# A one-layer language-model tower: two-pass attention scores on whole-number rows, and a new order of a turn

## The reference, cut to what matters

```python
def _L0_attn_ref(x, Wq, bq, Wk, bk, Wv, bv, Wo, bo, gamma, beta):
    q = jnp.einsum('bsd,dhk->bshk', x, Wq) + bq
    k = jnp.einsum('bsd,dhk->bshk', x, Wk) + bk
    v = jnp.einsum('bsd,dhk->bshk', x, Wv) + bv
    scores = jnp.einsum('bqhk,bshk->bhqs', q, k) * scale
    attn = jax.nn.softmax(scores, axis=-1)
    ctx = jnp.einsum('bhqs,bshk->bqhk', attn, v)
    attn_out = jnp.einsum('bqhk,hkd->bqd', ctx, Wo) + bo
    y = x + attn_out
    return (y - mu) * jax.lax.rsqrt(var + EPS) * gamma + beta      # mu, var of y

h = _L0_tok_ref(x, mask, ...)                 # embedding, window features, fusion, layer norm
h = h + _L0_attn_ref(_layernorm(h), ...)
h = h + _L0_ffn_ref(_layernorm(h), ...)       # top-2 gate, each expert takes 64 rows, GELU
return h
```

## Time and profile before

| what | value |
|---|---|
| median of 3 runs | 537.13 us |
| lowest and highest of the runs | 536.72 and 547.7 us |
| time of the profiled execution | 537.01 us |
| its span, from the first to the last instruction | 535.2 us |
| mean granted TensorE clock, as a share of full speed | 0.989 |
| TensorE matmul busy (share of the span) | 497.3 us (93%) |
| DVE busy | 447.9 us (84%) |
| GpSimd busy | 384.7 us (72%) |
| ScalarE busy | 379.2 us (71%) |

### The profile page before, as it was taken

How to read it: one execution, slowest core, us unless ns; L and a number is a source line. 1 busy time by engine, 2 the same in 40 slices (tenths; PEclk the granted TensorE clock), 3 DMA queues, 4 the chain that set the end, 5 groups by cost and what they waited for, 6 DMA issues and landing times. The chain is left out here.

```text
span 535.2 us, 15239 instructions
## 1 busy us (share of the span) xinstructions
PE 497.3 (93%) x5567; PEld 362.8 (68%) x5567; DVE 447.9 (84%) x1054; ACT 379.2 (71%) x768; POOL 384.7 (72%) x519
## 2 busy tenths in 40 slices
PE   5988799999999999999999998769999999999984
PEld 3876567777777777776777775534466767777664
DVE  4797669999999999998999999868778898878675
ACT  2868778888898888988898887336766555556530
POOL 1025669888788888888888888750468798789783
PEclk9998989999999999999999999999999999999998
DMA  6800000000000000000000000000734163351011
GB/s 233 333 6 2 2 2 4 2 3 3 3 2 3 3 3 3 4 2 4 3 4 2 3 3 2 2 1 4 168 80 100 23 150 76 77 138 38 31 40 60
DMA packets 11902, 21.68 MB, mean 41 GB/s; under 512 B 4668, under 2 KB 9780, under 8 KB 10164
## 3 DMA queue, kind: packets, MB, share of 16 engines
q1 hardware_dynamic: 11410, 20.15, 13.8%
q10 hardware_dynamic: 418, 0.55, 0.4%
HBM read 16.24 MB, written 4.33 MB: 38 GB/s over the span
## 5 line engine op out<-in xcount | busy, mean ns | idle before, releaser
L845 POOL TENSOR_TENSOR s_pl<-s_pf,s_ph 128x512 f16<-128x512 f32 x128 | 147.0, 1160 | 8.7 <-ACT s_ph L959 8.7
L1062 DVE TENSOR_REDUCE s_mx<-ps 128x4 f32<-128x512 f32 x128 | 83.8, 677 | 17.6 <-PE ps L1225 14.1
L953 ACT ACTIVATE s_pf<-ps,s_ln_r 128x512 f32<-128x512 f32 x128 | 87.1, 683 | 11.4 <-PE ps L1238 8.9
L823 PE MATMUL ps<-s_xt_all,s_w1s 128*128 128x512 f16 x384 | 87.9, 379 | 2.2 <-ACT s_ub L1543 1.6
L1698 PE MATMUL ps<-s_w2s,s_hid 128*128 128x256 f16 x768 | 88.9, 273 | 0.0
L1698 PEld LDWEIGHTS ps<-s_w2s,s_hid 128*128 128x128 f16 x768 | 75.1, 98 | 11.0
L959 ACT ACTIVATE s_ph<-s_pf 128x512 f16<-128x512 f32 x128 | 74.0, 637 | 0.0
L1273 PE MATMUL ps<-s_zh,s_cth 128*128 128x256 f16 x256 | 69.9, 273 | 1.0 <-DVE s_ctl L1096 1.0
L1273 PE MATMUL ps<-s_zl,s_cth 128*128 128x256 f16 x256 | 69.8, 273 | 0.0
L1273 PE MATMUL ps<-s_zh,s_ctl 128*128 128x256 f16 x256 | 69.8, 273 | 0.0
L823 PEld LDWEIGHTS ps<-s_xt_all,s_w1s 128*128 128x128 f16 x384 | 37.3, 98 | 41.4 <-ACT s_ub L1543 2.1
(11 more groups left out here) (246 smaller groups left out, 1149.0 us busy)
## 6 DMA issues: line engine op xcount, KB each, us to landing
s_rep<-picks SPq DMA_DIRECT2D x14, 512.0 KB, 6.7
s_stage<-in_w SPq DMA_DIRECT2D x2, 1024.0 KB, 14.3
out<-s_zh SPq DMA_DIRECT2D x16, 128.0 KB, 2.0
out<-s_lg SPq DMA_DIRECT2D x16, 128.0 KB, 1.7
s_stage<-in_wq SPq DMA_DIRECT2D x1, 1024.0 KB, 5.0
s_stage<-in_wk SPq DMA_DIRECT2D x1, 1024.0 KB, 6.7
s_stage<-in_wv SPq DMA_DIRECT2D x1, 1024.0 KB, 8.3
s_stage<-in_wo SPq DMA_DIRECT2D x1, 1024.0 KB, 10.8
```

What stands on the lines that cost most here:

```text
L823: mm = nc.tensor.matmul(hidden_bank(n)[:], w1s[:, wp, c, j * P:(j + 1) * P], xt_all[:, GB * g:GB * (g + 1), xp, c, :], start=(k == 0), sto ...
L845: nc.gpsimd.tensor_tensor(flat(pl[:, b % 2, 4 * j:4 * j + 4, :]), pf[:, j, :], flat(ph[:, b % 2, 4 * j:4 * j + 4, :]), ALU.subtract).then_ ...
L953: nc.scalar.activation(pf[:, j, :], ST[j % 2][:], ACT.Exp, bias=ln_r[:, b:b + 1]).then_inc(exp_done[j], 1)
L1062: nc.vector.tensor_reduce(mx[:, b % 2, c:c + 4], A[ab][:].rearrange("p (h k) -> p h k", h=4), AX.X, ALU.max).then_inc(max_done[hf][ab], 1)
```

## The change

The three passes of `score_cols` become two. The stationary operand is no longer the scaled `ub` in two parts but `nkT`, the transposed whole-number counts, which one float16 holds exactly. The key's scale moves into the exponential, as `scale=r12` of the activation. Three scale vectors are carried as pairs of rows (a float16 and its rest), so the row numbers `ONE` and `SHIFT` move, and `SHIFT` is now two rows. The transfers of `mrow` become four in a turn instead of two.

`nkT` is made in block one: eight `nkt_part` groups of eight matmuls, which take the place of both stretches of `keep_going`, four copies on ScalarE and four on DVE. The copy of `nb` to `nk` on ScalarE moves to behind the wo biases. The scale rows of `nkT` are filled at the start of block two: four small matmuls (`scale_rows`), one copy on DVE, and twelve transfers of 32 rows of 256 bytes each on SyncE's queue, ahead of the first `mrow` transfers.

The order of a turn changes on three engines. On TensorE `score_rows(i+3, 1)` now stands behind `residual(i)` where `score_rows(i+4, 1)` stood at the end of the turn, the second half of `q_rows` comes first, and `maxima_cols` stands between the two halves. On ScalarE `q_hi(1)` comes before `max_row`, and `probs_hi(1)` moves to the start of the next turn. On DVE both `q_lo` are at the start of the turn and `y_scaled` comes before the second half's `sum_root`.

```diff
-R2, ONE, SHIFT = 2 * V, 2 * V + 1, 2 * V + 2
-ONE_HI, UV = R2 + 2, R2 + 4
+R2, ONE, SHIFT = 2 * V, 2 * V + 2, 2 * V + 4
+UV = ONE + 2
...
+                def nkt_cols(n):
+                    dve.wait_ge(nt_ready, 8 + n + 1)
+                    nc.vector.tensor_copy(nkT[:, 16 + 4 * n:20 + 4 * n, :].rearrange("p b t -> p (b t)"), NKT_BANKS[4 + n][:])\
+                        .then_inc(nkt_ok, 1)
...
+                sp.wait_ge(srow_step, 2)
+                for ab in range(2):
+                    for r, j in ((R2, 0), (R2 + 1, 1), (ONE, 2), (ONE + 1, 3), (SHIFT, 2), (SHIFT + 1, 3)):
+                        r += ab * UD
+                        sp.dma_start(nkT[r:r + 1, :, :], srow[:, j, :]).then_inc(in_srow, 16)
                 for b in range(B):
                     sp.wait_ge(mrow_done, b + 1)
                     for ab in range(2):
-                        r = ab * UD + SHIFT
-                        sp.dma_start(qh[r:r + 1, b % 2].rearrange("o f t q -> o (f t) q"),
-                                     mrow[8 * ab:8 * ab + 8, b % 2, :]).then_inc(shift_in[b % 2], 16)
+                        for r in range(ab * UD + SHIFT, ab * UD + SHIFT + 2):
+                            sp.dma_start(qh[r:r + 1, b % 2].rearrange("o f t q -> o (f t) q"),
+                                         mrow[8 * ab:8 * ab + 8, b % 2, :]).then_inc(shift_in[b % 2], 16)
...
-                    nc.scalar.activation(pf[:, j, :], ST[j % 2][:], ACT.Exp, bias=ln_r[:, b:b + 1]).then_inc(exp_done[j], 1)
+                    nc.scalar.activation(pf[:, j, :], ST[j % 2][:], ACT.Exp, bias=ln_r[:, b:b + 1], scale=r12[:, b:b + 1]).then_inc(exp_done[j], 1)
...
 # ScalarE's order of a turn
+                    if has(i + 2) and i > -2:
+                        probs_hi(i + 2, 1)
                     if has(i + 1):
                         context_hi(i + 1, 0)
+                    if has(i + 2):
+                        exps(i + 2, 3)
...
                     if has(i + 4):
-                        q_hi(i + 4, 0)
+                        q_hi(i + 4, 1)
...
                     elif has(i + 3):
                         max_row(i + 3)
-                    if has(i + 2):
-                        exps(i + 2, 3)
                     if has(i + 4):
-                        q_hi(i + 4, 1)
+                        q_hi(i + 4, 0)
...
                 def score_cols(b, hf):
                     if hf == 0:
-                        pe.wait_ge(shift_in[b % 2], 32 * (b // 2) + 32)
+                        pe.wait_ge(shift_in[b % 2], 64 * (b // 2) + 64)
+                        if b == 0:
+                            pe.wait_ge(in_srow, 16 * 12)
...
-                    for n, (part, q) in enumerate(((0, qh), (0, ql), (1, qh))):
+                    for n, q in enumerate((qh, ql)):
                         for ab in range(2):
                             r = slice(ab * UD, ab * UD + UD)
-                            mm = nc.tensor.matmul(ST[ab][:], ub[r, b, part, :], flat(q[r, b % 2, hf]),
-                                                  start=(n == 0), stop=(n == 2))
+                            mm = nc.tensor.matmul(ST[ab][:], nkT[r, b, :], flat(q[r, b % 2, hf]),
+                                                  start=(n == 0), stop=(n == 1))
...
 # TensorE's order of a turn
+                scale_rows()
                 for i in STEPS:
                     if has(i):
                         residual(i)
+                    if has(i + 3):
+                        score_rows(i + 3, 1)
+                    tokens(i - 1, 2)
+                    if has(i - 1):
+                        logits(i - 1)
                     if has(i + 1):
+                        values(i + 1, 1)
                         turn(i + 1, 0)
-                        values(i + 1, 1)
                     if i == B:
                         first_hidden(4)
-                    if has(i - 1):
-                        logits(i - 1)
+                    if has(i + 2):
+                        score_cols(i + 2, 1)
                     if i == -3:
                         maxima_cols(0)
                     if has(i + 4):
-                        q_rows(i + 4, 0)
-                    if has(i + 2):
-                        score_cols(i + 2, 1)
+                        q_rows(i + 4, 1)
                     if has(i + 3) and i > -3:
                         maxima_cols(i + 3)
+                    if has(i + 4):
+                        q_rows(i + 4, 0)
                     if has(i + 1):
                         turn(i + 1, 1)
-                    if has(i + 4):
-                        q_rows(i + 4, 1)
...
-                    if has(i + 4):
-                        score_rows(i + 4, 1)
-                    tokens(i, 2)
```

More of the change, by code:

```diff
@@ L581, in _, with nkt_part @@
                         mm.then_inc(nt_ready, 1)
-                keep_going(15, psum[0][:, 0:FREE])
+                def nkt_part(n):
+                    if 1 <= n < 4:
+                        pe.wait_ge(nt_ok, (1, 2, 4)[n - 1])
+                    elif n >= 4:
+                        pe.wait_ge(nt_ok, 4 + (2, 3, 1, 4)[n - 4])
+                    for k in range(4):
+                        for ab in range(2):
+                            mm = nc.tensor.matmul(NKT_BANKS[n][ab * UD:(ab + 1) * UD, k * P:(k + 1) * P], nb[:, 4 * n + k, :], ident16[:],
+                                                  start=True, stop=True)
+                    mm.then_inc(nt_ready, 1)
+                for n in range(4):
+                    nkt_part(n)
                 pe.wait_ge(in_id, 16)
@@ L590, in _ @@
                 tp.then_inc(mt_ready, 1)
-                keep_going(6, psum[0][:, 0:FREE])
+                nkt_part(4)
+                nkt_part(5)
                 pe.wait_ge(mt_ok, 1)
@@ L1137, in _ @@
                         q_lo(i + 5, 1)
[L1138 to L1139 removed]
+                        q_lo(i + 5, 0)
+                    if i == -4:
+                        log_rho()
+                    elif i < -4:
+                        for n in DVE_TOKENS.get((i, 0), ()):
+                            token_rows(n)
                     if has(i + 2):
                         context_lo(i + 2, 1)
[L1142 to L1143 removed]
                     if has(i + 3):
@@ L1166, in _ @@
                         sums(i + 3, 1)
-                    if has(i + 1) and i % 4 == 2:
-                        logits_out((i + 1) // 4)
+                    if has(i + 2):
+                        y_scaled(i + 2)
                     if has(i + 3):
@@ L1171, in _ @@
                         context(i + 3, 1)
-                    if has(i + 2):
-                        y_scaled(i + 2)
-                    if has(i + 3):
                         context_lo(i + 3, 0)
-                    if has(i + 6):
-                        q_lo(i + 6, 0)
                     if has(i + 2):
@@ L1300, in logits, with scale_rows @@
                     mm.then_inc(lg_ready, 1)
+                def scale_rows():
+                    for j in range(4):
+                        mm = nc.tensor.matmul(MISC[0:B, j * P:(j + 1) * P], nk[:, :, R2 + j:R2 + j + 1].rearrange("p b o -> p (b o)"),
+                                              identh[:], start=True, stop=True)
+                    mm.then_inc(srow_step, 1)
                 def maxima_cols(b):
+                    if b == 0:
+                        pe.wait_ge(srow_step, 2)
                     for n in range(2):
```

80 lines of the change are left out of this document (49 added, 31 removed).

## The result

The changed kernel takes 589.16 us (median of 4 runs, 583.69 to 594.37) against 539.67 for the kernel before, a ratio of 1.090 (95% interval 1.077 to 1.104). Its profiled execution took 583.69 us, with a span of 581.9.

The account below looks back on a forecast made before the run. The prediction took SyncE's queue of four transfers to set a 9.63 us turn: 537.0 profiled + 33.0 for thirty turns + 1.1 block one + 0 start + 0.8 last sequence = 571.9, so 572 us; range 557 to 600.

Parts of the forecast that it names:

- the queue's loop: From `q_rows(1)` over SyncE's four `mrow` transfers and the scores to the next `q_rows(1)`: 9.63 us a turn; 74%.
- 30 ordinary turns against 8.53: Turns between second and last `mrow`: each 1.10 us longer, 33.0 us in all.
- up to the second `mrow`: Block one +1.1 us, for four DVE copies ahead of `quads`; start of block two counted 0.
- last `mrow` to the router's transposes: The last sequence: `max_row` to scores grows from 2.88 to 4.08 us; less two passes, +0.8.
- X: Landing time from the start of the last `mrow` issue to the scores: 1.75 us, possible from 1.30 to 2.10.
- both "hidden" rivals: The four transfers don't set the turn: DVE's loop does, 535 us (9%), or a shorter DVE loop, 525 us (5%).
- `q_rows(1)` to `q_hi(1)`: First step of the queue's loop, until ScalarE's input is ready: 0.65 us.
- the clock falls: TensorE's clock falls for good through its 1.5 us stall in every turn: over 750 us; 3%.
- the slow start: Twelve scale-row transfers in block two cost up to 2.7 us each and hold the first scores: 594 us; 9%.
- GpSimd's at 8.50: Old turn's loop from `residual` through GpSimd to `x_cols` and back: 8.50 us, falling to 8.08 with the change.
- DVE's at 8.40: Old turn's loop from `score_rows(1)` through DVE's maxima and `context_lo(0)` to `output(0)` and back: 8.40 us, unchanged.
- TensorE alone: TensorE's own loop of starts in a turn: 8.50 us before, 8.06 with one pass less in each half.

Follow-up runs that it names:

- before_four: The kernel before, with each `mrow` transfer issued twice, the extra one to a tile nobody reads: four transfers in a turn; ratio 1.072, turn 9.70 to 9.71 us.
- after_one_row: The changed kernel with two `mrow` transfers in a turn, leaving out the low part of the row maxima's scale: 538.4 us, ratio 0.9997, turn 8.44.
- after_two_queues: The changed kernel with two of the four `mrow` transfers issued by ScalarE right behind `max_row`: 582.8 us, ratio 1.083, turn 9.89.
- after_const_scale: The changed kernel with a constant instead of the column of key scales in the exponentials: 578.9 us, ratio 1.074, turn 9.68.
- after_one_row_best: `after_one_row` with `max_row` ahead of `q_hi(1)` and `first_hidden(4)` ahead of the last `logits`: 528.6 us, ratio 0.982, turn 8.22.
- before_residual_first: The kernel before with only `score_rows(1)` moved behind `residual`, three passes and two transfers: 540.5 us, ratio 1.004, turn 8.56.

## Why the prediction was right, and where its size was off

The forecast was 572 us, slower, by the queue's loop; it came out slower, inside the range, by that loop. The profiled execution took 583.7, so 11.8 more than the sum. The turn of 9.77 instead of 9.63 comes from one mis-sized term; most of the rest was not in the sum at all:

| part | forecast | measured | off by |
|---|---|---|---|
| 30 ordinary turns against 8.53 | 33.0 | 30 x 1.24 = 37.2 | +4.2 |
| irregular turns | 0 | 301.0 - 293.1 = 7.9 | +7.9 |
| up to the second `mrow` | +1.1 | 66.14 - 68.88 = -2.7 | -3.8 |
| last `mrow` to the router's transposes (at 411.0, before 364.7) | +0.8 | 43.9 - 40.0 = +3.9 | +3.1 |
| the rest | 0 | 170.9 - 170.5 = +0.4 | +0.4 |

- *The queue's terms held.* 128 transfers, 0.63 to issue the median one, four in 2.64; X was 1.76 where I took 1.75. `before_four` and `after_one_row` show that they are the cause, and both "hidden" rivals fall.
- *The rule of the Trainium skill.* "DMA: Bandwidth & Descriptors", section "Issuing engines are not separate DMA queues", calls the time to start a DMA usually small relative to the DMA. The measured turn doesn't agree for transfers this small: 0.66 against a landing of 1.76. The same section's other half, that a second engine saves just this time on the sequencer, agrees with `after_two_queues`, where two queues issued side by side (1.30 and 1.40 for two each).
- *Mis-sized: `q_rows(1)` to `q_hi(1)`.* I took 0.65; it was 0.79. The exponential that stands between them got the scale column and takes 778 ns instead of 689. I costed only the passes, transfers and orders of the diff, and not the operand it added to `exps`. `after_const_scale` gives back 0.09. The page "ScalarE: Activation LUTs", section "What ACT_TABLE_LOAD costs", states about 93 ns for each column operand; the trace agrees with 0.09.
- *Missed: irregular turns.* The forecast took an ordinary turn times 30. Before, most of a late transfer fell into slack, and 30 turns cost 0.85 more than 30 x 8.50 in all. Now nothing covers it: what lands late is added in full, and behind three of the pauses the clock was halved for some microseconds, 1.6 more in each of the two turns of 12.4. The rival "the clock falls" priced a fall for good; what happened was a fall in single turns.
- *Start.* Here the prediction named the gain ("could even give back 2") and counted 0. Each of the twelve scale rows took 0.59 to issue, under even the lower price, so the slow start fell as a rival. Block one grew by 0.6 and not by 1.1 (`quads` at 21.11 instead of 20.51), and with the earlier `log_rho` the first exponentials came at 60.35 instead of 62.50.
- *End: overlooked.* The new order also puts the last `logits` ahead of `first_hidden(4)`. In the changed kernel (PEq is TensorE's instruction sequencer):

```profile
400.41 0.31 PE L1343 MATMUL ps<-s_wgs,s_xt_all 128*128 128x16 f16 x6 [1.01 <-DVE s_xt_all L1159]
400.57 2.65 PE L857 MATMUL ps<-s_xt_all,s_w1s 128*128 128x512 f16 x6
...
403.54 0.22 DVE L760 TENSOR_TENSOR s_stage<-s_lg,s_bg_b 128x64 f32<-128x64 f32 x1 [2.57 <-PEq L862]
```

Before, the hidden tile filled the time until `x_lo` was ready:

```profile
355.07 1.46 PE L823 MATMUL ps<-s_xt_all,s_w1s 128*128 128x512 f16 x6
...
357.26 0.23 DVE L727 TENSOR_TENSOR s_stage<-s_lg,s_bg_b 128x64 f32<-128x64 f32 x1 [0.33 <-PEq L828]
```

Now TensorE waits first and then does the same tile in 2.65 instead of 1.46, and all engines wait for it at the block's end. The six matmuls are the same; the longer time is the clock's, which was at 0.51 over the tile, where it was 1.00 over the tile before:

```profile
400.60:403.30 2.70, 2.62 (x11) 0.67 (x7) 0.22 (x1) 0.00 (x0) 0.00 (x0) 0.51 0.00 0
```

The same fall stands in `after_one_row` (0.50 from 355.3 to 358.0). With that step put back (`after_one_row_best`), the last stretch went from 42.8 in `after_one_row` to 39.2: 3.6 less, where I had expected 2.3. The tile took 1.46 again, which is 1.2 of the 3.6. In the changed kernel the clock fell once more in this stretch (0.50 from 387 to 390), which the kernel before doesn't show.
- *The other loops.* GpSimd's at 8.50 and DVE's at 8.40 were read as lengths of loops. GpSimd's rested on 0.42 of idle weight load ahead of `x_cols`, taken for a wait. The changed kernel has the same 0.42 where `xc` had been ready for 1.65:

```profile
232.72 0.20 PEld L1333 LDWEIGHTS ps<-s_ident,s_xc 128*128 128x128 f32 x2 [0.42 <-issue]
```

In both kernels `x_cols` starts 0.31 behind the last matmul pass of the scores (234.04 to 234.35 before, 232.41 to 232.72 after), so GpSimd cost nothing there before; its loop was near the turn (`xc` ended 0.07 ahead) but isn't shown to have set it. DVE's was too long: `before_residual_first` should have had 8.62 by it and had 8.56 with DVE idle ahead of its maxima, and in `after_one_row_best` it closes at 8.22 at most. TensorE alone was too short at 8.06, if 8.56 with three passes is its length in the new order. And ScalarE's loop was missing from the list: `after_two_queues` is what that costs. None of this touched the forecast, because the queue's loop was far above them all, but it decides what is left to win.
- *The range.* Its lower end follows from X at 1.30. Its upper end of 600 is worked out nowhere: 22 for the slow start on top of 572 is 594, and on top of 582 it is 604. Nothing hangs on it here: the measured time lies inside either.

## What to carry to other kernels

A small transfer in a loop costs its issue on the queue, one after the other, and then its landing; count both for every transfer, beside the step that it is moved past. Before a saved pass is credited, list a loop for each engine and for each queue, and price every operand that the diff adds to an instruction in one of them. Where a loop with a DMA loses its slack, every late landing is added in full: leave room there, or expect more than the ordinary turn times the number of turns. An idle time in front of an instruction is a wait only if it shrinks when its releaser comes earlier.

## What the runs showed of the hardware that I had not expected

- A second column operand (scale beside bias) makes an exponential of 128x512 0.09 us longer: 689 to 778 ns.
- ScalarE did nothing else while it issued transfers: 1.40 for two, 1.54 idle.
- After pauses of 2.02, 2.40 and 2.46 us in otherwise full work TensorE's granted clock fell to half, and came back by itself. After pauses of 2.04 and 3.17 it stayed at 1.00, and so it did in the ordinary turn with 1.39 in each.
- The four late landings of the changed kernel (2.36 to 3.50 after the last issue) all came in turns in which a packet of an instruction queue was under way; the other 27 lay within 0.03 of each other, five of them with such a packet too.
- Of the twelve transfers of scale rows the landing took 1.8 us at least, 1.9 in the middle and 3.5 at most:

```profile
DMA to landing us min/median/max: 1.8/1.9/3.5
```
